# TensorE's side work in the stages with heads of 16: only in the second tick of a pair

## The reference

```python
scores = jnp.einsum('bhqd,bhkd->bhqk', qh, kh) * scale      # qh, kh, vh: 16 heads of 16
attn = jax.nn.softmax(scores, axis=-1)
out = jnp.einsum('bhqk,bhkd->bhqd', attn, vh)
return out.transpose(0, 2, 1, 3).reshape(B, LQ, D_MODEL) @ Wo + bo
```

## Time and profile before

| | us |
|---|---|
| median of 3 runs (4139.22 to 4171.97) | 4162.28 |
| the profiled execution | 4162.91 |
| its span, first to last instruction | 4161.1 |
| TensorE busy | 2881.4 (69%) |
| VectorE busy | 1882.4 (45%) |
| ScalarE busy | 1478.3 (36%) |
| GpSimd busy | 966.3 (23%) |

### The profile page before, as it was taken

How to read it: one execution, slowest core, us unless ns; L and a number is a source line. 1 busy time by engine, 2 the same in 40 slices (tenths; PEclk the granted TensorE clock), 3 DMA queues, 4 the chain that set the end, 5 groups by cost and what they waited for, 6 DMA issues and landing times. The chain is left out here.

```text
span 4161.1 us, 40121 instructions
## 1 busy us (share of the span) xinstructions
PE 2881.4 (69%) x14574; PEld 1626.0 (39%) x14580; DVE 1882.4 (45%) x3010; ACT 1478.3 (36%) x1967; POOL 966.3 (23%) x1019
## 2 busy tenths in 40 slices
PE   4889974578594577775837678757997985882233
PEld 2333333323263333333723233246786872330112
DVE  3554544466344333231653333244324224653798
ACT  1455553156421243332413344333333322661111
POOL 2132221122232144344021223330000001222233
PEclk7799986789787788887867888878999996995555
DMA  5355530155200344442014444300111114531000
GB/s 124 77 117 114 120 79 27 41 114 110 60 1 24 89 118 109 116 105 63 1 47 118 116 108 123 89 27 16 57 35 47 46 40 80 113 87 47 1 8 12
DMA packets 179748, 294.09 MB, mean 71 GB/s; under 512 B 47136, under 2 KB 71712, under 8 KB 179360
## 3 DMA queue, kind: packets, MB, share of 16 engines
q1 hardware_dynamic: 134496, 221.89, 22.8%
q0 software_dynamic: 45056, 69.64, 6.2%
HBM read 185.39 MB, written 105.91 MB: 70 GB/s over the span
## 5 line engine op out<-in xcount | busy, mean ns | idle before, releaser
L1499 DVE TENSOR_REDUCE L_mx<-bank_t 128x2 f32<-128x1024 f32 (+3 forms) x512 | 560.0, 1122 | 484.2 <-PE bank_t L1328 305.6
L1695 ACT ACTIVATE L_P<-bank_t 128x1024 f32<-128x1024 f32 (+2 forms) x512 | 477.5, 949 | 429.0 <-PE bank_t L1347 279.5
L1499 DVE TENSOR_REDUCE L2a_mx<-bank_t 128x2 f32<-128x1024 f32 x256 | 312.0, 1224 | 689.2 <-PE bank_t L1328 689.2
L1695 ACT ACTIVATE L2a_P<-bank_t 128x1024 f32<-128x1024 f32 x256 | 262.2, 1024 | 439.1 <-PE bank_t L1347 438.8
L1328 PE MATMUL bank_t<-L2a_KS,L2a_QS 96*128 96x512 f32 x512 | 232.0, 544 | 245.6 <-DMA L2a_KS<-L2a_spill_k_halves 154.0
L1328 PE MATMUL bank_t<-L_KS,L_QS 48*128 48x512 f32 (+2 forms) x1024 | 251.2, 493 | 98.3 <-DMA L_QS<-L_spill_q_halves 77.3
L1347 PE MATMUL bank_t<-L_QS,L_KS 50*128 50x512 f32 (+2 forms) x1024 | 235.5, 464 | 116.9 <-DVE L_mx L1499 104.3
L1372 PE MATMUL bank_o<-L2a_P,ones 128*32 128x512 f32 x1024 | 290.0, 645 | 0.0
L1368 PE MATMUL bank_o<-L_P,L_V 128*32 128x512 f32 (+3 forms) x2048 | 273.5, 608 | 4.9 <-ACT xn L1699 3.3
L1328 PEld LDWEIGHTS bank_t<-L2a_KS,L2a_QS 96*128 96x128 f32 x512 | 98.2, 218 | 371.4 <-issue 360.7
L1328 PEld LDWEIGHTS bank_t<-L_KS,L_QS 48*128 48x128 f32 x1024 | 105.9, 205 | 309.5 <-issue 218.8
(11 more groups left out here) (426 smaller groups left out, 5847.9 us busy)
## 6 DMA issues: line engine op xcount, KB each, us to landing
L_KS<-L_spill_k_halves SPq DMA_DIRECT2D x192, 128.0 KB, 4.3
L_QS<-L_spill_q_halves SPq DMA_DIRECT2D x192, 128.0 KB, 4.6
L2a_KS<-L2a_spill_k_halves SPq DMA_DIRECT2D x96, 256.0 KB, 8.5
L2a_QS<-L2a_spill_q_halves SPq DMA_DIRECT2D x96, 256.0 KB, 5.4
L_spill_raw<-xn POOLq DMA_DIRECT2D x64, 256.0 KB, 2.5
L2a_spill_raw<-xn POOLq DMA_DIRECT2D x64, 256.0 KB, 2.9
L2g_raw<-in_L_ffn_h_blocks SPq DMA_DIRECT2D x32, 512.0 KB, 3.6
L_spill_k_halves<-L_hi SPq DMA_DIRECT2D x32, 256.0 KB, 2.0
```

The source lines that it names most:

```text
L1499: e.tensor_reduce(neg, s.tile[:, :, 0:n_keys], AX.X, ALU.max, negate=True).then_inc(sem(s.done), 1)
L1695: e.activation(s.at.Pr[s.pb][:, :, q0:S], s.tile[:, :, q0:S], ACT.Exp, scale=s.at.scale).then_inc(sem(s.exp), 1)
```

## The change

`run_due` takes an argument that says whether a chore may run in this tick. The main loop of `attention` passes true only in the last tick of a step (p = GP - 1). With heads of 32 there is one tick per step (GP = 1), and nothing changes. With heads of 16 (GP = 2) every chore that fell in a first tick now runs in the second tick of the same pair, one tick later.

```diff
-            def run_due(gapped=True):
+            def run_due(gapped=True, chore=True):
@@
-                if chores and (not gapped or tick[0] - last_chore[0] >= gap):
+                if chores and chore and (not gapped or tick[0] - last_chore[0] >= gap):
@@
-                            run_due()
+                            run_due(chore=p == at.GP - 1)
```

## The result

| | before | after |
|---|---|---|
| median of 8 runs each, us | 4149.99 (4139.22 to 4171.97) | 4197.93 (4171.01 to 4214.77) |
| the profiled execution, us | 4162.91 | 4205.59 |
| its span, us | 4161.1 | 4203.8 |
| mean granted clock of TensorE | 0.818 | 0.802 |

The changed kernel is slower: ratio 1.0105, 95% interval 1.007 to 1.0141. A second comparison gave 1.0095 (1.0064 to 1.0125). That is about 1%, on the edge of what the prediction called no change: 47.9 us between the medians of the table, 38.7 us in the second comparison.

The account below looks back on a forecast made before the run. Bound: TensorE, busy 83 to 90% in the changed stretches; only its idle time could be won. 4162.9 - 28.4 + 31.5 = 4166.0, less 2 us for first units: 4164 us, range 4122 to 4204.

Parts of the forecast that it names:

- main case: VectorE wait goes, a wait for the stack of queries comes, some clock falls; chance 0.72, 4140 to 4190 us.
- slower rival: Each new wait for the stack brings a clock fall as long as L1's: 4195 us, chance 0.15.
- the wait for VectorE: Logits waits until VectorE frees the previous tick's Smax tile: 35.3 us in L0, 34.3 in L1, falling to about 20 in L1.
- The net gain of 28.4 us: 9.7 us less in L1, 9.7 in L3, 9 in L0, with no fall of the clock in L1 and L3.
- the slow unit: One L1 unit before the change, behind the wait at 999.94: 37.8 us, 6.9 more than 30.93.
- the term for the values' projection: Each moved part of the values' projection saves 0.93 us, as a keys' projection does; six parts in L1.
- the chain: Queries' projection through ScalarE, GpSimd, HBM write and read to the unit's first Smax: 20.83 us, making 30.93 per unit.
- Three new waits: Waits for the stack of queries: 3 of 2 us or more in L1, 3 in L3, 3 more than before in L0.
- the size of a fall: Clock fall behind each of nine new stack waits: between 0 and 6.9 us, taken as 3.5, together 31.5 us.
- The chain gives way: Rival: the stack of queries is ready sooner and the pairs' 41 us come through, 4122 us; chance 0.13.

Follow-up runs that it names:

- before again: The kernel before, unaltered, run once more for its profile and clock: 4157.12 us (one run).
- after again: The changed kernel, unaltered, run once more against the kernel before: 4193.38 us, ratio 1.0095.

## Why the prediction was right or wrong

4164 us was forecast and 4198 measured: inside the range of 4122 to 4204, 34 us above the value, outside the main case's own 4140 to 4190, and by the ratio, 1.05%, just on the slower side of the bound that the prediction set at 1%. The sum started from the profiled execution, 4162.9 us, while the median of eight before is 4149.99: the change of the time was forecast at +1 us and measured at +48. So it is luck that the value came within 34 us, and 4198 lies in the range only by the room that was left for the slower rival.

**The balance.** Means of three profiles on each side (before, before again and the stage left unchanged in a kernel with half the change; after, after again and the changed stage of such a kernel), from the stretches of the stages. TensorE is busy 490.0 us in L0 before and 527.2 after, 228.1 and 234.9 in L1, 228.0 and 235.7 in L3: 51.7 more. It is idle 71.9 and 64.1, 63.9 and 60.8, 57.9 and 57.0: 11.8 less. That makes 39.9 us, against 47.9 and 38.7 between the medians.

**Right: the wait for VectorE.** Foreseen from 34.3 to about 20; measured 19.2 in L1, 17.8 in L3, 19.6 in L0. The pair with the queries' projection took 4.92 us, where 4.93 was worked out.

**The net gain of 28.4 us: right in the idle time, wrong in the clock.** 13.8 us of it, 6.9 in L1 and in L3, was the slow unit that the prediction put down to a fall of the clock and took to be gone; the other 14.6 us was idle time. Measured are 11.8 us less of idle time, so that part came nearly true. The 13.8 us did not come: TensorE is busy 6.8 and 7.7 us longer in L1 and L3. Within the idle time the term for the values' projection failed ("as long as a keys' projection, so 0.93 too"): in the new place two parts wait up to 3.0 us for VectorE to empty bank_m, 5.2 us in L1. The trace of before had that wait at the start of the stage (5.8 us in two, from 802 to 1098 us) and could have warned.

**Right: the chain, wrong: that it sets the period.** From projection to first Smax the four units of L1 took 21.4, 22.5, 21.4 and 21.7 us; 20 to 21 was foreseen. But only one of them waited (3.09 us), since between the two points TensorE took longer than the 18.60 us foreseen. In two of the other three units a wait for VectorE to empty bank_m stands there (3.0 and 2.2 us); in the third TensorE was busy for 18.45 of 20.50 us (987.7 to 1008.2) at a clock of 1.00. Three new waits were counted for L1, three for L3 and three for L0. L3 has its three (11.2 us in four waits, 1.6 in one before; 6 to 10 us was foreseen for L1 and L3), L1 has one of 3.1 us, and L0 has 11.6 us in five against 10.4 in six.

**Wrong: the size of a fall.** This is the step: "I take the middle, 3.5, because L0's fall is as deep but an L0 unit has less work at half speed." In L1 and L3 it holds roughly: behind the new waits the falls last 3.4 to 13.7 us, and about half of a fall is lost. So falls stay short there although the neighbours are parted; why L0 differs is open. In L0 the term was wrong by far: 3 x 3.5 = 10.5 us was counted, and TensorE is busy 37.2 us longer. At units 5, 9 and 13 the falls last 109.2, 61.5 and 105.8 us together in the three profiles with the change in L0, and 20.4, 27.2 and 17.0 in the three without. The means are 92.2 and 21.5; half of the difference of 70.7 us is 35 us, the most that these three falls can explain of the 37.2. All falls that begin in L0 sum to 215 us in the mean with the change and to 120 without, so three quarters of the growth is at the three units. These falls are not new. They stood in the trace of before (the earlier trace rows shows one), cost 2 to 5 us each (half their length), and the sum counted only new falls.

**Wrong: the reason against the slower rival**, "in second ticks TensorE has fewer idle gaps with which to stay at 1.2 GHz." It stayed there for 61.4 us, busy for 61.0 of them. The rival itself, at 0.15, gave 4195 us, close to the time; its clock term of 9 x 6.9 = 62 us compares with 51.7 measured, but its mechanism, each new wait with a fall as long as L1's, is not what happened: in L0, where most of the loss is, hardly a wait is new, and the old falls at units 5, 9 and 13 last about four times as long. That its value came close is luck.

The prediction weighed the rule of the Trainium skill's "TensorE: Matmul & The Clock Gate", What's actually happening, that activity releases the throttle, as speaking for the change where it packs chores closer. The trace does not agree that being busy is enough: the clock was 0.50 through 61.4 us of which TensorE was busy for 61.0. The 3.8 us in the rival "The chain gives way" is an estimate from figures that the Trainium skill gives in "DMA: Bandwidth & Descriptors", Anatomy of one DMA, for one transfer issued by GpSimd. The read here is six transfers issued by SyncE, and after the change it took 7.79 us again (932.01 to 939.80).

## What to carry to other kernels

Where a kernel is near a fall of the clock, look in the trace for what stands in the stretches at whose end the clock comes back, and try to keep it together; a change of order that saves idle time can lengthen every fall that was there already. Sum such a change over the falls that exist, not only over new ones. And cost a wait from the tile's reader at the new place: work that is moved out of one engine's shadow may fall into another's.

## What the runs showed of the hardware

- TensorE can stay at 1.2 GHz while busy 99% of the time: 61.0 of 61.4 us, in two different kernels at two different units.
- In L0, behind waits of nearly the same length (1.7 to 4.3 us), the falls at units 5, 9 and 13 were 3.4 to 17.1 us or 20.5 to 61.4 us, by whether the values' matmuls (over 128 rows) and the next chore stood side by side or with a Smax and a Logits of 48 and 50 rows between them. Behind a wait of 6.00 us one lasted 20.5 us with them side by side. What it is in that neighbourhood that matters was not measured.
- A wait of 1.38 to 1.74 us can be followed by a fall, and one of 1.9 us (unit 13 with the change in L1 and L3 alone) by none.
